# Two kinds of product packed in a four-layer transformer kernel: last-quarter tokens of two sequences side by side, and softmax sums inside the value product

## What is computed

```python
x = rms_norm(hidden_states, ln_in_w)
mixed = jnp.where(vm, x @ v_qkv, x @ l_qkv)             # vm: this token and the next have type 1
q, k = apply_rotary(q, k, position_ids, l)
ctx = sdpa(q, k, v, causal=True)                        # 16 heads of 16, softmax(q k) v
hidden_states = residual + jnp.where(vm, ctx @ v_dense, ctx @ l_dense)
cctx = sdpa(cq, ck, cv, causal=False)                   # 16 heads of 8, against 64 memory rows
hidden_states = hidden_states + cctx @ cdense_w
mi = rms_norm(hidden_states, ln_post_attn_w)            # the feed-forward, inner width 688
v_out = jax.nn.silu(mi @ v_gate) * (mi @ v_up) @ v_down
l_out = jax.nn.silu(mi @ l_gate) * (mi @ l_up) @ l_down
hidden_states = hidden_states + jnp.where(vm, v_out, l_out)
```

## Time and profile before

| | |
|---|---|
| median of 3 runs | 1439.62 us |
| the profiled execution | 1439.24 us |
| its span, first to last instruction | 1437.5 us |
| mean granted TensorE clock | 0.985 |
| PE, DVE, ACT, POOL busy | 1383.1, 791.9, 501.0, 349.7 us |

### The profile page before, as it was taken

One profiled execution on the slowest core, in us unless ns is written; L12 is line 12 of the kernel. 1 busy time (PEld: TensorE's weight loads), 2 busy tenths in 40 slices (PEclk: granted clock), 3 DMA queues, 4 the chain that ended last, 5 costly groups with the idle time before them and its releaser, 6 DMA issues.

```text
span 1437.5 us, 27076 instructions
## 1 busy us (share of the span) xinstructions
PE 1383.1 (96%) x11507; PEld 1116.1 (78%) x11507; DVE 791.9 (55%) x1490; ACT 501.0 (35%) x845; POOL 349.7 (24%) x382
## 2 busy tenths in 40 slices
PE   7988799999999999999999999999899999999998
PEld 5866578787787788888888888776678788787776
DVE  4555686766666665443333433245676665756653
ACT  3333332423423322244434544333341332423321
POOL 1243342222323120111011111224332323222210
PEclk9998999999999999999999999989999999999999
DMA  9010000000010001200000000011000000000000
GB/s 317 2 59 1 2 2 2 1 1 2 1 45 2 2 23 34 98 1 0 1 0 1 0 1 1 1 40 41 2 2 9 2 9 9 2 8 5 6 8 16
DMA packets 19906, 27.36 MB, mean 19 GB/s; under 512 B 3432, under 2 KB 15552, under 8 KB 19520
## 3 DMA queue, kind: packets, MB, share of 16 engines
q1 hardware_dynamic: 19008, 24.20, 5.1%
q10 hardware_dynamic: 768, 1.26, 0.3%
HBM read 23.35 MB, written 2.10 MB: 18 GB/s over the span
## 4 chain that ended last, share of the span: by engine, by line
PE 90%; DVE 4%; ACT 2%; issue 1%; POOL 1%; DMA 0%; SPq 0%; POOLq 0%; ACTq 0%; DVEq 0%
PE bank L1234 15%; PE bank L1259 8%; PE bank L1122 6%; PE bank L975 5%; PE bank L1458 4%; PE row_banks L1105 4%; PE bank L1465 4%; PE row_banks L1365 4%; PE bank L1422 4%; PE row_banks L1072 4%; PE bank L1040 3%; PE bank L968 3%; PE row_banks L1077 2%; PE row_banks L1394 2%; PE row_banks L1319 2%; PE bank L1201 2%
## 5 line engine op out<-in xcount | busy, mean ns | idle before, releaser
L1606 ACT ACTIVATE room<-bank 128x256 f32<-128x256 f32 x176 | 66.8, 383 | 218.4 <-PE bank L1234 169.3
L1811 DVE TENSOR_REDUCE room<-row_banks 128x4 f32<-128x512 f32 (+1 forms) x128 | 116.7, 954 | 46.7 <-PE row_banks L1077 46.5
L1234 PE MATMUL bank<-room,gate_w 128*128 128x256 f32 (+1 forms) x640 | 135.9, 335 | 5.1 <-DVE room L1898 2.2
L1895 DVE SCALAR_TENSOR_TENSOR room<-room,bank 128x256 f32<-128x256 f32 x176 | 73.3, 417 | 107.1 <-ACT room L1606 106.9
L1234 PE MATMUL bank<-room,up_w 128*128 128x256 f32 (+1 forms) x640 | 130.9, 327 | 0.0
L1576 ACT ACTIVATE room<-row_banks 128x1536 f32<-128x1536 f32 x64 | 92.9, 1452 | 102.7 <-PE row_banks L1105 102.7
L1259 PE MATMUL bank<-room,down_w 128*128 128x256 f32 (+1 forms) x704 | 128.5, 332 | 0.0
L840 POOL TENSOR_SCALAR_AFFINE_SELECT room<-room 128x1024 f32<-128x1024 f32 x64 | 71.1, 1110 | 216.7 <-ACT room L1576 216.7
L1234 PEld LDWEIGHTS bank<-room,gate_w 128*128 128x128 f32 x640 | 98.5, 190 | 32.2 <-issue 18.0
L1259 PEld LDWEIGHTS bank<-room,down_w 128*128 128x128 f32 x704 | 109.8, 191 | 9.9 <-issue 0.7
L1234 PEld LDWEIGHTS bank<-room,up_w 128*128 128x128 f32 x640 | 103.0, 191 | 8.3
(11 more groups left out here) (228 smaller groups left out, 2642.1 us busy)
## 6 DMA issues: line engine op xcount, KB each, us to landing
out_x<-wq SPq DMA_DIRECT2D x8, 256.0 KB, 2.2
qkv<-in_L_xattn_v_qkv SPq DMA_DIRECT2D x2, 768.0 KB, 6.1
qkv<-in_L_xattn_l_qkv SPq DMA_DIRECT2D x2, 768.0 KB, 8.9
gate_w<-in_L_xattn_v_gate SPq DMA_DIRECT2D x2, 640.0 KB, 8.8
gate_w<-in_L_xattn_l_gate SPq DMA_DIRECT2D x2, 640.0 KB, 7.6
up_w<-in_L_xattn_v_up SPq DMA_DIRECT2D x2, 640.0 KB, 6.3
up_w<-in_L_xattn_l_up SPq DMA_DIRECT2D x2, 640.0 KB, 6.5
down_w<-in_L_xattn_v_down SPq DMA_DIRECT2D x2, 640.0 KB, 6.5
```

The costliest lines, as they stand in the source:

```text
L1234: last = pe.matmul(b[:, j * S + lo:j * S + hi], w[:, k, f * P:(f + 1) * P], y[:, k, lo:hi], start=(k == 0), stop=(k == KT - 1))
L1811: last = dve.tensor_reduce(dst, row_banks[:, :, P * i:P + S * i], X, ALU.max, negate=True)
```

## The change

**Last-quarter tokens in pairs.** The vision tiles of the feed-forward no longer run for each sequence. POOL copies the last 64 columns of both sequences of a pair side by side (`late_y`), and after the odd one's language tiles PE does the five vision tiles for 128 columns at once (`late_up` in three groups of 2, 2 and 1 tiles, `late_down` into bank3), with their own `late_tanh`, `late_hidden` and `late_give`. For early vision tokens the run-time branch now stands inside each half of a language tile, both experts share one hidden tile, and POOL splits it (`by_expert`, two passes over 192 columns for each of five tiles, always executed). `up` and `down` have six steps a sequence in place of eleven.

**Values padded with ones.** A head's values have 16 columns; the other 16 of its group of 32, zero before, are now ones. One product thus gives values on 16 rows and sums on the other 16, and the products with the constants are gone. The even head of a pair has its sums on the odd head's rows and goes to one half of the bank, the odd head to the other half. ACT copies the even half out, once masked for its sums and once for its values (`apart`, two passes); DVE adds the odd half's sums and values by two masked scalar_tensor_tensor, turns the sums by 16 rows (`stream_shuffle` with `OTHER`), takes the reciprocal and multiplies. The cross-attention gets the same. `values(e, 1)` waits for ACT's copies of `values(e, 0)`.

**Order and buffers.** All tables of times are new, so all engines' orders are; the output has two buffers; the two sequences of a pair are turned out together at the end of their pair.

```diff
+OTHER = [(i + HD) % 32 for i in range(32)]
...
-put(12.1998, "values", 0)
...
+put(542.3948, "values", 0)
+put(542.5531, "second_scores", 2)
+put(543.0906, "values", 1)
...
+pool.memset(v_pads, 1.0)
+pool.memset(mot_zero, 0.0).then_inc(pads_zero, 1)
...
+def late_y(e):
+    pool.wait_ge(*CRS_DVE.did(e, "yv"))
+    if e >= 2:
+        pool.wait_ge(*FF_PE.did(e // 2 * 2 - 1, "vup2"))
+    pool.tensor_copy(ff_late[:, :, e % 2, :], ff_yv[:, :, LATE:]).then_inc(*FF_POOL.does(e, "late"))
+
+def by_expert(e, i):
+    pool.wait_ge(*FF_DVE.did(e, f"hid{i}"))
+    pool.tensor_tensor(hid_v[:, i, :], hid[:, i, 0:LATE], seen(e)[:, 0:LATE], ALU.mult)\
+        .then_inc(*FF_POOL.does(e, f"hv{i}"))
+    pool.wait_ge(*FF_POOL.did(e, f"hv{i}"))
+    pool.tensor_tensor(hid[:, i, 0:LATE], hid[:, i, 0:LATE], hid_v[:, i, :], ALU.subtract)\
+        .then_inc(*FF_POOL.does(e, f"hl{i}"))
...
-        pe.wait_ge(*ATT_DVE.did(e, "ctx0"))
-    half = const[:, C_HALF + 32 * par:C_HALF + 32 * par + 32]
-    for at, of_sums in ((0, False), (S, True)):
-        for i in range(TT):
-            for j in range(4):
-                last = pe.matmul(att_bank[32 * j:32 * j + 32, at + i * P:at + S],
-                                 half if of_sums else v_pad[e % 2][:, i, 8 * t + 2 * j + par, :],
-                                 probs[w % 2][:, j, S * i:S + P * i],
-                                 start=(par == i == at == 0), stop=(par == i == 1),
-                                 skip_group_check=True)
+        pe.wait_ge(*ATT_DVE.did(e, "vals0"))
+    if par == 1:
+        pe.wait_ge(*ATT_ACT.did(e, f"own{t}"))
+    for i in range(TT):
+        for j in range(4):
+            last = pe.matmul(att_bank[32 * j:32 * j + 32, par * S + i * P:par * S + S],
+                             v_pad[e % 2][:, i, 8 * t + 2 * j + par, :], probs[w % 2][:, j, S * i:S + P * i],
+                             start=(par == i == 0), stop=(i == 1), skip_group_check=True)
...
-        pair = const[:, C_PAIR + 32 * h:C_PAIR + 32 * h + 32]
-        for at, of_sums in ((0, False), (S, True)):
-            for g in range(4):
-                last = pe.matmul(crs_bank[32 * g:32 * g + 32, at:at + S],
-                                 pair if of_sums else cv_pad[:, 2 * g + h, :], c_probs[:, g, h, :],
-                                 start=(h == at == 0), stop=(h == 1), skip_group_check=True)
+        for g in range(4):
+            last = pe.matmul(crs_bank[32 * g:32 * g + 32, h * S:(h + 1) * S], cv_pad[:, 2 * g + h, :], c_probs[:, g, h, :],
+                             start=(h == 0), stop=True, skip_group_check=True)
...
-    def columns(y, lo, hi):
-        for j, w in enumerate((gate_w, up_w)):
-            for k in range(KT):
-                last = pe.matmul(b[:, j * S + lo:j * S + hi], w[:, k, f * P:(f + 1) * P],
-                                 y[:, k, lo:hi], start=(k == 0), stop=(k == KT - 1))
-        return last
-
-    if f < FULL:
-        with pe.If(has_early[e % B]):
-            columns(ff_yv, 0, LATE)
-        last = columns(ff_yv, LATE, S)
-    elif f < 2 * FULL:
-        last = columns(ff_yl, 0, S)
-    else:
-        for m, w in enumerate((gate_w, up_w)):
+    for m, w in enumerate((gate_w, up_w)):
+        if f < 2 * FULL:
+            out = b[:, m * S:(m + 1) * S]
+            pe.matmul(out, w[:, 0, f * P:(f + 1) * P], ff_yl[:, 0, :], start=True, stop=False, skip_group_check=True)
+            with pe.If(has_early[e % B]):
+                for k in range(KT):
+                    pe.matmul(out[:, 0:LATE], w[:, k, i * P:(i + 1) * P], ff_yv[:, k, 0:LATE],
+                              start=False, stop=False, skip_group_check=True)
+            last = pe.matmul(out, w[:, 1, f * P:(f + 1) * P], ff_yl[:, 1, :], start=False, stop=True, skip_group_check=True)
...
+def late_up(e, g):
+    if g == 0:
+        pe.wait_ge(*FF_POOL.did(e - 1, "late"))
+        pe.wait_ge(*FF_POOL.did(e, "late"))
+    pe.wait_ge(*FF_DVE.did(e, ("hid4", "hid5", "vhid0")[g]))
+    b = ff_bank[(g + 1) % 2]
+    for j, f in enumerate(LATE_TILES[g]):
+        for m, w in enumerate((gate_w, up_w)):
+            for k in range(KT):
+                at = (2 * j + m) * P
+                last = pe.matmul(b[:, at:at + P], w[:, k, f * P:(f + 1) * P],
+                                 ff_late[:, k].rearrange("p e n -> p (e n)"), start=(k == 0), stop=(k == KT - 1))
+    last.then_inc(*FF_PE.does(e, f"vup{g}"))
...
+    f = FULL + i
+    if i == 0:
+        pe.wait_ge(*FF_DVE.did(e, "vhid1" if e % 2 else "hid5"))
+    pe.wait_ge(*(FF_POOL.did(e, f"hl{i}") if i < FULL else FF_DVE.did(e, f"hid{i}")))
+
+    def whole(t):
+        return pe.matmul(ff_bank[0][:, t * S:(t + 1) * S], down_w[:, f, t * P:(t + 1) * P],
+                         hid[:, i, :], start=(i == t == 0), stop=(i == UPS - 1), skip_group_check=True)
+
+    whole(0)
+    if i < FULL:
+        with pe.If(has_early[e % B]):
+            for t in range(KT):
+                pe.matmul(ff_bank[0][:, t * S:t * S + LATE], down_w[:, i, t * P:(t + 1) * P], hid_v[:, i, :],
+                          start=False, stop=False, skip_group_check=True)
+    whole(1).then_inc(*FF_PE.does(e, f"down{i}"))
+
+def late_down(e, g):
+    pe.wait_ge(*FF_DVE.did(e, "vhid2"))
+    for f in LATE_TILES[g]:
         for t in range(KT):
-            last = pe.matmul(ff_bank[0][:, t * S + lo:t * S + hi], down_w[:, f, t * P:(t + 1) * P],
-                             hid[:, f, lo:hi], start=(i == t == 0), stop=(i == NF - 1),
-                             skip_group_check=True)
-        return last
-
-    if f < FULL:
-        with pe.If(has_early[e % B]):
-            columns(0, LATE)
-        last = columns(LATE, S)
-    else:
-        last = columns(0, S)
-    last.then_inc(*FF_PE.does(e, f"down{i}"))
+            last = pe.matmul(ff_bank[1][:, t * P:(t + 1) * P], down_w[:, f, t * P:(t + 1) * P], hid_late[:, f, :],
+                             start=(f == t == 0), stop=(f == FULL - 1), skip_group_check=True)
+    last.then_inc(*FF_PE.does(e, f"vdown{g}"))
...
+def apart(e, t):
+    act.wait_ge(*ATT_PE.did(e, f"pv{2 * t}"))
+    if t == 1:
+        act.wait_ge(*ATT_DVE.did(e, "turn0"))
+    elif e > 0:
+        act.wait_ge(*ATT_DVE.did(e - 1, "turn1"))
+        act.wait_ge(*ATT_POOL.did(e - 1, "cl"))
+    act.activation(recip, att_bank[:, 0:S], ACT.Copy, scale=keep(1)).then_inc(*ATT_ACT.does(e, f"oth{t}"))
+    act.activation(ctx_sb[:, t, :], att_bank[:, 0:S], ACT.Copy, scale=keep(0)).then_inc(*ATT_ACT.does(e, f"own{t}"))
+
+def cross_apart(e):
+    act.wait_ge(*CRS_PE.did(e, "cpv"))
+    act.activation(c_recip, crs_bank[:, 0:S], ACT.Copy, scale=keep(1)).then_inc(*CRS_ACT.does(e, "coth"))
+    act.activation(c_ctx, crs_bank[:, 0:S], ACT.Copy, scale=keep(0)).then_inc(*CRS_ACT.does(e, "cown"))
...
+    dve.wait_ge(*ATT_ACT.did(e, f"own{t}"))
     dve.wait_ge(*ATT_PE.did(e, f"pv{2 * t + 1}"))
-    if e > 0 and t == 0:
-        dve.wait_ge(*ATT_POOL.did(e - 1, "cl"))
-    dve.reciprocal(recip, att_bank[:, S:2 * S]).then_inc(*ATT_DVE.does(e, f"rec{t}"))
+    bank = att_bank[:, S:2 * S]
+    dve.scalar_tensor_tensor(recip, bank, keep(0), recip, ALU.mult, ALU.add).then_inc(*ATT_DVE.does(e, f"sums{t}"))
+    dve.scalar_tensor_tensor(ctx_sb[:, t, :], bank, keep(1), ctx_sb[:, t, :], ALU.mult, ALU.add)\
+       .then_inc(*ATT_DVE.does(e, f"vals{t}"))
+    dve.wait_ge(*ATT_DVE.did(e, f"sums{t}"))
+    dve.stream_shuffle(turned_sums, recip, OTHER).then_inc(*ATT_DVE.does(e, f"turn{t}"))
+    dve.wait_ge(*ATT_DVE.did(e, f"turn{t}"))
+    dve.reciprocal(turned_sums, turned_sums).then_inc(*ATT_DVE.does(e, f"rec{t}"))
     dve.wait_ge(*ATT_DVE.did(e, f"rec{t}"))
-    dve.tensor_tensor(ctx_sb[:, t, :], att_bank[:, 0:S], recip, ALU.mult).then_inc(*ATT_DVE.does(e, f"ctx{t}"))
+    dve.tensor_tensor(ctx_sb[:, t, :], ctx_sb[:, t, :], turned_sums, ALU.mult).then_inc(*ATT_DVE.does(e, f"ctx{t}"))
...
+def late_hidden(e, g):
+    gate, up = late_banks(g)
+    h = late_hid(g)
+    dve.wait_ge(*FF_ACT.did(e, f"vtanh{g}"))
+    dve.scalar_tensor_tensor(h, h, 1.0, gate, ALU.add, ALU.mult).then_inc(*FF_DVE.does(e, f"vsilu{g}"))
+    dve.wait_ge(*FF_DVE.did(e, f"vsilu{g}"))
+    dve.tensor_tensor(h, h, up, ALU.mult).then_inc(*FF_DVE.does(e, f"vhid{g}"))
+
+def late_give(e):
+    dve.wait_ge(*FF_PE.did(e, "vdown2"))
+    dve.wait_ge(*FF_DVE.did(e, "x4"))
+    for k, done in ((0, "xv0"), (1, "xv")):
+        x, late = late_of(e, k), ff_bank[1][:, k * P:(k + 1) * P].rearrange("p (e s) -> p e s", e=2)
+        dve.scalar_tensor_tensor(x, late, 0.5, x, ALU.mult, ALU.add).then_inc(*FF_DVE.does(e, done))
```

729 lines of the change are left out of this document (395 added, 334 removed).

## The result

The changed kernel takes 1435.93 us (median of 20 runs, 1433.05 to 1437.54), the one before 1439.57 beside it: ratio 0.9965, 95% interval [0.9956, 0.9975]. The gain is 3.6 us where 51 were forecast, and the time lies outside the range. The profiled execution spans 1435.6 us against 1437.5. In the experiments two executions, of 2594.5 and 2190.0 us, lie far from all others of their kernels and are left out of the medians.

A forecast was written before the change was run, and what follows sets the result against it. PE, busy 96% of the span, was taken to bound the kernel. 1437.5 - 110 (work) + 65 (waits) - 6 (small gains and costs) = 1386.5, with 1.7 us outside the span 1388 us; range 1345 to 1415.

The forecast's parts named there:

- rival C: Rival, 4%: waits thin PE until the chip grants a lower clock in the two layers too, +113 us, 1501 us.
- (3): Ends of layers: `dense` of the last sequences waits for DVE's chain; layer 1 gives 16.5, layer 3 21, together +37 us.
- What goes: Work leaving PE at full clock: feed-forward -50, attention values -46, cross values -14 us; sum -110.
- (1): Scores and exp: score stages wait on the banks, 1.6 us in even sequences, 0.6 in odd; +13 us.
- (2): Dense and the norm's sum: a wait of 0.5 to 0.9 us for six sequences in two layers; +8 us.
- (4): Late products between language tiles and down, and longer cross context: about 0.5 us for each of eight pairs, +4.
- (5): First two sequences of each layer: PE already waited for exp, `context` is longer; 12 of 46 us not had, +12.
- POOL "no bound": POOL gains 160 passes of up to 0.72 us, near +100 on 350 us, and was called no bound.
- The small gains: Last feed-forward's waits for `hidden` -3, weight load idle at a waiting branch -4, outputs at the end +1 us.
- D: Rival, 4%: 240 feed-forward branches each leave PE idle 0.2 to 0.25 us, +50 to 60, 1440 to 1450 us.
- The lock: DVE and POOL exclude each other; each of 48 last multiplies in `context` may wait up to 0.7 us, mostly in slack.
- B: Rival, 14%: all walked waits and more, as DVE's passes and POOL delay; 85 to 95 us come back, 1410 to 1420.

## Why the prediction was wrong

The sum had -110 for work, +65 for waits and -6 for small things, -51. It came to -100, +70 and +27.5. Of the 49 us by which that missed, 27.5 are a term that I priced at nothing, 10 lie in the work, and 11 in waits and small gains.

- **The step that failed is the clock's.** The sum has no term for it. It stands only in rival C, which I priced as all 890 us of the layers at the clock of one idle stretch (24% idle, 0.87) and gave 4%. What came is neither that nor nothing: 27.5 us, 16 of them behind the first `give`, at single places. One wait of 3 us was enough in seven cases of eight, and my own term (3) forecast such waits at four places. I should have asked what stood before each fall of the clock in the trace of before, not what its mean was. By the rule of the Trainium skill that I had quoted there, TensorE: Matmul & The Clock Gate, "HAM oscillation — how this bites in real kernels", the long waits of (3) were the likely places; the trace agrees, with 0.92 and 0.91 in those windows.
- **What goes.** Feed-forward -50: -55. Attention values -46: -38, since the stage is 0.79 to 0.82 and not 0.72 us, and was 1.41 on average. Cross values -14: -13. That is 106; some 6 came back, 3.5 in the mask products of the first scores (L1077, now L1156) and 2.5 in the norms' sums (L987, now L1066), which have as many instructions as before; why is not shown.
- **(1), (2) and (4)**, the steady parts, +25: +23 (10.0 and 15.2 against 0.9 and 1.0). Right, with waits of 0.5 to 0.9 us at the second scores among them. The run without sums shows that (1) comes from the missing work.
- **(3), ends of layers**, +37: +28 (13.3 and 24.5 against 1.8 and 8.2). Cause right (DVE's `context` ahead of what PE needs), place wrong: it is `memory`, which waits for `rl` behind `context`, and takes part of the wait from `dense` (2.7 us in sequence 15, not 4 and more in all four). It was oversized (and the waits listed for layer 3 come to 22, not 21), and is still the largest, with 14 us of clock beside it.
- **(5)**, first sequences, +12: +19 (the start and the stretch to layer 3's first `give`), and 10 of clock, in part perhaps chance.
- **POOL "no bound"**: false where it counts. 100 us more busy time would have fitted, but `by_expert` waits in its queue: 7 us. I had listed POOL's gain by time alone and had not asked what is queued behind its waits.
- **The small gains** of 6: the last feed-forward's waits of 0.55 us went, but one of 2.8 ahead of its first tile came. The branches cost nothing that I can see (D out).
- **The lock**: the last multiply of `context` took 425 ns, now 610 in the mean, and the four passes over x_all (L1767, now L1880) 709 in place of 533, 23 us in all. 9 of these 23 us went with `by_expert` (638), the others not, and the multiply kept its 610 (627).
- The rivals: B had the right sort (all walked waits and more) but no clock; the time lies above it. I had priced each wait, and treated 110 us of removed work as had until a wait was found for it; the three runs that changed work alone, with every other engine and the order as they were, gave 35 to 55% of it back to idle time and clock (by their profiled executions).

Not settled: what starts each of the other stretches at 1.2 GHz in the first 200 us, and whether part of them is chance; and what the best order for this work would give, since only nine places were moved. Nor is it known how close together short waits must stand for the clock to fall.

## What to carry to other kernels

Price a wait of an otherwise full TensorE by its length in one piece: here a pause of 3 us cost near 5, and waits of 1 us or less, 13 us apart, only themselves; several of 0.4 to 1.3 us close together were also followed by half clock. Of work taken from the engine that bounded, a third to a half came back here as waits even where no chain got longer, and 70 us of 100 in the whole change, where one did. A pass given to an idle engine still stands in that engine's queue: look for what stands behind its waits.

## What was not expected of the hardware

- A single pause of 2.8 to 3.1 us of TensorE, between stretches without a wait, was followed by 1.2 GHz in seven cases of eight; 16 pauses of 0.7 to 1.1 us and 32 of 0.8 or less by none. The record turned 1.7 to 4.3 us after the start of such a pause. Two or three waits of 0.4 to 1.3 us close together were followed by it too, at three places of the changed kernel.
- Skipped branches in a row on TensorE: 12 stop it for 3.0 us, 7 for 0.7 to 1.1, 3 for 0.8 or less.
- The product of 128 x 256 f32 used as a filler takes 0.43 us, two instructions of 0.216 in the records; I had counted one.
- Kernels that do the same in their first 200 us (the one before, and those with pauses) lost 8 to 18.5 us there to the clock. What sets that isn't known.
